# Two loads of each step issued from ScalarE's queue, earlier in the step, instead of from SyncE's

## The reference

```python
xn = layernorm(x)                       # over the 256 columns, no scale or shift
x = x + attention(xn) + ffn(xn)
# attention: 16 heads of 16; segments of 512 rows; keys and values are every 8th row
# of a segment (64 keys); for each block of 64 queries the maximum over the block is
# subtracted per key, then exp; num = w @ v, den = sum(w) + 1e-10; out = (num/den) @ Wout.T
# ffn: relu(xn @ W1 + b1) @ W2 + b2, with an inner width of 1024
```

## Time and profile before

| | |
|---|---|
| median of 3 runs | 1063.42 us (1061.55 to 1066.39) |
| the profiled execution, its own time | 1065.93 us |
| its span, first to last instruction | 1064.1 us |
| granted TensorE clock, mean | 0.998 |
| TensorE busy | 1041.9 us, 98% |
| VectorE busy | 841.3 us, 79% |
| ScalarE busy | 648.2 us, 61% |
| GpSimd busy | 623.6 us, 59% |
| share of 16 DMA engines taken by SP's queue | 73.3% |

### The profile page before, as it was taken

One profiled execution on the slowest core, in us unless ns is written; L12 is line 12 of the kernel. 1 busy time (PEld: TensorE's weight loads), 2 busy tenths in 40 slices (PEclk: granted clock), 3 DMA queues, 4 the chain that ended last, 5 costly groups with the idle time before them and its releaser, 6 DMA issues.

```text
span 1064.1 us, 19176 instructions
## 1 busy us (share of the span) xinstructions
PE 1041.9 (98%) x5381; PEld 810.6 (76%) x5381; DVE 841.3 (79%) x1465; ACT 648.2 (61%) x1080; POOL 623.6 (59%) x489
## 2 busy tenths in 40 slices
PE   5999999999999999999999999999999999999998
PEld 4676787777787777877777877777877777877777
DVE  7878888878887788888878788788877878887753
ACT  5656666666656566565666656666666665656663
POOL 6346556656656556556655656565565565556564
PEclk9999999999999999999999999999999999999999
DMA  5457777778776878777778877778768787767754
GB/s 193 98 156 207 210 214 206 206 215 227 222 209 184 228 202 244 211 194 198 214 224 225 221 204 196 219 214 235 216 191 214 202 232 211 212 176 217 196 145 146
DMA packets 153577, 216.38 MB, mean 203 GB/s; under 512 B 27345, under 2 KB 96721, under 8 KB 153553
## 3 DMA queue, kind: packets, MB, share of 16 engines
q1 hardware_dynamic: 153408, 215.96, 73.3%
q10 hardware_dynamic: 144, 0.13, 0.0%
HBM read 100.41 MB, written 58.46 MB: 149 GB/s over the span
## 4 chain that ended last, share of the span: by engine, by line
PE 88%; DVE 4%; DMA 3%; SPq 2%; issue 1%; ACT 1%; DVEq 0%; ACTq 0%
PE h_bank L1027 38%; PE y_bank L1027 38%; PE s_banks L1102 5%; PE misc L1209 3%; PE s_banks L1209 2%; PE misc L1027 2%; DMA k_pack<-k_dram 1%; DMA w_exp<-w 1%; DVE xn L828 1%; DVE s_max L845 1%; SPq L382 1%; DVE w_exp L851 1%; DMA yt_dram<-y_mem 0%; DVE q_lo L894 0%; SPq L407 0%
## 5 line engine op out<-in xcount | busy, mean ns | idle before, releaser
L540 POOL TENSOR_TENSOR h_lo<-h_full,h_hi 128x512 fp32r<-128x512 f32 x256 | 337.4, 1319 | 376.0 <-ACT h_full L621 372.6
L627 ACT ACTIVATE w_exp<-w_exp 128x512 f32<-128x512 f32 x256 | 161.6, 633 | 252.7 <-DVE w_exp L851 251.0
L619 ACT ACTIVATE h_hi<-h_bank,b_cols 128x512 fp32r<-128x512 f32 x256 | 174.8, 683 | 65.3 <-PE h_bank L1027 59.5
L1027 PE MATMUL h_bank<-xt_hi,w_hi 128*128 128x512 f32 x512 | 206.3, 403 | 0.0
L1027 PE MATMUL h_bank<-xt_lo,w_hi 128*128 128x512 f32 x512 | 199.9, 391 | 0.0
L1027 PE MATMUL h_bank<-xt_hi,w_lo 128*128 128x512 f32 x512 | 199.6, 390 | 0.0
L845 DVE TENSOR_REDUCE s_max<-s_banks 128x8 f32<-128x512 f32 x254 | 170.9, 673 | 29.1 <-PE s_banks L1102 28.8
L1027 PE MATMUL y_bank<-h_hi,w_hi 128*128 128x512 f32 x496 | 193.6, 390 | 0.2 <-ACT w_exp L627 0.2
L1027 PE MATMUL y_bank<-h_hi,w_lo 128*128 128x512 f32 x496 | 193.3, 390 | 0.0
L1027 PE MATMUL y_bank<-h_lo,w_hi 128*128 128x512 f32 x496 | 193.3, 390 | 0.0
L851 DVE TENSOR_TENSOR w_exp<-s_banks,s_max 128x512 f32<-128x512 f32 x254 | 175.7, 692 | 11.0
(11 more groups left out here) (141 smaller groups left out, 1538.5 us busy)
## 6 DMA issues: line engine op xcount, KB each, us to landing
q_pack<-q_hi SPq DMA_DIRECT2D x248, 128.0 KB, 2.5
rden_rows<-rden_dram SPq DMA_DIRECT2D x128, 128.0 KB, 4.6
x_b<-x SPq DMA_DIRECT2D x32, 512.0 KB, 4.6
x_raw<-x SPq DMA_DIRECT2D x31, 512.0 KB, 4.8
q_pack<-q_lo SPq DMA_DIRECT2D x124, 128.0 KB, 2.4
yt_dram<-y_mem SPq DMA_DIRECT2D x124, 128.0 KB, 3.5
y_mem<-yt_dram SPq DMA_DIRECT2D x31, 512.0 KB, 4.5
out<-x_b SPq DMA_DIRECT2D x31, 512.0 KB, 3.1
```

The costliest lines, as they stand in the source:

```text
L540: pool.tensor_tensor(h_part[1][:, i % HBUF], h_full[:, i % HBUF], f32(h_part[0][:, i % HBUF]), ALU.subtract).then_inc(h_lo, 1)
L619: act.activation(h_part[0][:, i % HBUF], h_bank[i % 2][:], ACT.Relu, bias=b1_cols[:, i:i + 1]).then_inc(h_hi, 1)
L627: act.activation(w_exp[:, pair], w_exp[:, pair], ACT.Exp).then_inc(w_ready, 1)
L1027: mm = pe.matmul(ps, stationary[a], moving[b], start=start and c == 0 and n == 0, stop=stop and c == len(pairs) - 1 and n == 2, skip_group ...
```

## The change

The loads of x for statistics (`load_x` and `load_keys` of the steps) and for the residual (`load_again`) leave SP's list and are issued by ScalarE on its own DMA queue: `load_next` after `hidden` at i = 3, `load_again` after `hidden` at i = 6. In the last step `load_again(31)` stands at i = 3; before, SP issued it at the end of step 30. GpSimd's `residual(31)` moves from i = 3 to i = 6. The loads of the first and lead step stay with SP. What each load waits for is the same as before.

```diff
 (SyncE)
-            def load_again(s, par):
-                sp.wait_ge(y_stored[par], (s - par) * 8)
-                sp.dma_start(x_b2[:, par], x_rows[s]).then_inc(x_again[par], 16)
...
-                if load:
-                    sp.wait_ge(xn_ready, s + 2)
-                    load_x(s + 3, 1 - par)
-                if load and par == 1:
-                    sp.wait_ge(xn_keys_ready, s + 3)
-                    load_keys(s + 3)
...
-                if ffn and not by_rows(s):
-                    load_again(s, par)
...
-                if attention and not norm:
-                    load_again(s + 1, 1 - par)
 (GpSimd)
-                    if i == 3 and by_rows(s):
+                    if i == 6 and by_rows(s):
                         residual(s, par)
 (ScalarE)
+            def load_next(s, par):
+                act.wait_ge(xn_ready, s + 2)
+                act.dma_start(x_raw[:, 1 - par], x_rows[s + 3]).then_inc(x_loaded[1 - par], 16)
+                if par == 1:
+                    act.wait_ge(xn_keys_ready, s + 3)
+                    act.dma_start(x_keys[:], x_key_rows[bass.ds((s + 3) * KEYS, P)]).then_inc(x_keys_loaded, 16)
+
+            def load_again(s, par):
+                act.wait_ge(y_stored[par], (s - par) * 8)
+                act.dma_start(x_b2[:, par], x_rows[s]).then_inc(x_again[par], 16)
...
                     if i in first:
                         hidden(past(s), first[i])
+                    if i == 3 and load:
+                        load_next(s, par)
+                    if i == (3 if by_rows(s) else 6):
+                        load_again(s, par)
```

## The result

The changed kernel takes 1097.07 us, the median of 4 runs (1090.75 to 1100.16), beside 1063.3 us for the kernel before in the same series. The ratio is 1.0291, with a 95% interval from 1.0264 to 1.0318. That is 33.8 us more (31 us by the ratio), where 1.5 us less was forecast, and far above the range's 1068.5 us. The profiled execution of after took 1090.75 us (span 1088.8 us, mean granted clock 0.994), the lowest of its four, so its rows show less of the loss than the median: 24.7 us of span.

What follows compares the result with a forecast made beforehand. TensorE bounds the kernel (88% of the span), so gains come only from idle time or clock. From the 1063.42 us median, 1.5 us off k_pack's waits and 0 elsewhere gave 1061.9 us, range 1058 to 1068.5.

Steps and rivals of the forecast that it cites:

- the new place of the transfers: Odd steps: x_raw and x_keys beside the store and xt_dram put off xt_dram's landing 0.8 to 1.6 us; worth 0.
- the cover: Slack in odd steps, 0.7 us before xt_hi plus 1.0 us before the first query product; TensorE feels delay from 1.7 us.
- The reload's early place: ScalarE at i = 6, ahead of k_hi: an issue of 0.4 to 0.6 us fits a 1.46 us wait; worth 0.
- Step 0: x_raw at 48 us instead of 54 meets q_pack, with TensorE idle around its keys; 0, up to +1 us.
- the loads put off the transposed rows: Rival, odd steps: xt_dram's delay stalls TensorE 0.4 to 1.2 us a step, 1075 us; 12% chance.
- The rule of turns between queues: DMA engines take queues in turn by packet, so xt_dram gets half a full engine while x_raw lasts; 1075 us.
- ScalarE's issue: Each load's issue on ScalarE takes 0.4 to 0.6 us, at most 1.47, and fits in its waits; worth 0.
- SP's 26 us: 75 load issues leave SP's queue, some 26 us of SP's time, which buys nothing by itself; worth 0.
- k_pack's waits: TensorE's 2.3 us of waits for k_pack shrink with two loads gone from before it; 1.5 us gained, 2.3 at best.
- The last step: residual between hidden_lo 6 and 7 leaves 0.6 us of cover; worth 0, bound +0.5 us.
- the sign by which it would be seen wrong: ScalarE's xt_hi waiting for xt_raw instead of for TensorE in odd steps would show the forecast wrong.

Runs made afterwards that it cites:

- e1: Changed kernel with the reload (x_b) back on SP at its old place, so only x_raw and x_keys are early on ScalarE; 1068.87 us, ratio 1.0047.
- e2: Changed kernel with x_raw and x_keys back on SP at their old places, so only the reload is early on ScalarE; 1074.97 us, ratio 1.0093.
- e5: Changed kernel with the reload moved from i = 6 to behind transposed_hi, which waits for xt_raw; 1070.52 us, ratio 1.0059.
- e13b: Changed kernel with the reload behind pair_keys_hi and a real wait for k_hi ahead of its issue; 1074.18 us, ratio 1.0086.
- e14b: Changed kernel with only x_keys (128 KB per odd step) back on SP behind xt_raw; 1067.41 us, ratio 1.0030.
- e4: Changed kernel with all loads still on ScalarE's queue but issued at about their old times, by waits for xt_dram's landing and k_lo; 1065.64 us, ratio 1.0017.
- e15: Changed kernel with x_keys and both loads of step 0 back on SP at their old places; 1064.15 us, ratio 0.9993.
- e16: Kernel before, with only x_raw's loads from step 1 on issued by ScalarE at i = 3; 1061.86 us, ratio 0.9975.
- e6: Changed kernel with ScalarE issuing the loads in even steps alone, SP as before in odd steps; 1067.57 us, ratio 1.0029.
- e11: All loads on SP's one queue, x_raw and x_keys ahead of xt_dram and the reload ahead of xt_raw; 1096.80 us, ratio 1.0299.
- e8: Changed kernel with a padded x_raw tile, so its loads go in pieces of 1 KB instead of 4 KB; 1091.28 us, ratio 1.0239.
- e7: Changed kernel with ScalarE issuing the loads in the odd steps alone; 1085.23 us, ratio 1.0207.
- e3: All loads on SP's one queue but early, x_raw and x_keys ahead of xt_dram and the reload right behind xt_raw; 1076.99 us, ratio 1.0116.
- e9: Changed kernel with the reload placed one instruction later in the program, behind pair_keys_hi, without a wait; 1095.79 us, ratio 1.0236.

## Why the prediction was wrong

**The step that failed** is the one on the new place of the transfers: "What does not fit, 0.8 to 1.6 us, puts off xt_dram's landing", "TensorE feels it from 1.7 us on, and the estimate stays just below. x_raw no longer runs beside xt_raw, which helps", "Worth 0". The delay itself was sized rightly, at the upper end: 1.6 us measured (5.00 to 6.61 us). That 1.6 us by itself stays within the cover is right as well: e1, with the same delay, loses 1.3 us at the query products in the whole kernel. What the step left out is what xt_raw then runs beside. The prediction moved x_b from 415.31 to about 410.2 in its own text, and xt_raw by up to 1.6 us from 407.49 to 409.1, and never set the two side by side. It also took an issue on ScalarE to start when the activation before it ends. The reload was issued 1.02 us ahead of k_hi, which is 409.14 on the old timeline, and so they meet, 0.56 us apart at most. xt_raw's landing, which it took as a constant 3.8 us, became up to 6.8 us, and both covers, 0.7 and 1.0 us, were used up. That x_raw no longer runs beside xt_raw didn't help: in e1's odd steps xt_raw lands in 3.9 us (median), in 3.7 before. That this meeting on top of the delay carries most of the loss is shown from five sides: the halves alone sum to 16.7 of 33.8 us (e1, e2), taking the reload away leaves 6.0 (e5), making it really later leaves about 10 (e13b), making xt_raw earlier under an unmoved reload leaves 3.4 (e14b), and a meeting with xt_raw on time costs 2.1 (e4).

**The reload's early place** was costed at nothing by way of its issue alone. Its bytes cost too: e2 shows 11.4 us through rden_rows, yt_dram and k_pack, transfers of which the prediction asked only whether something was taken from before them, not whether something was put there. But that price belongs to a reload beside the rows at their old place, and isn't a part of the 33.8 us: with x_raw early as well, and the meeting avoided, the early reload costs nothing that can be measured against before (e15), and some 2 us beside e16, which differs from e15 in the reload and the last step's residual (0.9975 against 0.9993, their intervals overlap).

**Step 0** was allowed 0 to +1 us and measured +2.8 us in q_pack's wait alone, 3 to 4 us by e6 and by e14b against e15. This is a term mis-sized, and the reason stood in the text ("x_raw at 48 us instead of 54 meets q_pack").

**The rival "the loads put off the transposed rows"** had the right chain (xt_dram, xt_raw, xt_hi, the query products in odd steps) and 12%. Its price, 0.4 to 1.2 us a step from a longer delay of xt_dram, was too low (18 us in the 13 odd steps of after's loop, up to 3.4 us in one), and its mechanism was not the whole: the xt_dram delay makes four tenths of the lateness in a stalled step (1.51 of 3.81 us in step 9), xt_raw's own landing the rest. The rule of turns between queues that stood beside it (the Trainium skill, DMA: Bandwidth & Descriptors, Queues, rings and completion order) is not needed for a late landing: e11's even steps have one on a single queue, where the reload stands ahead. And e8's store and xt_dram land no sooner for the smaller pieces beside them.

**What held.** ScalarE's issue is cheap: 0.34 us each, and less than its price in time, since here it starts while the hidden activation runs (342.31 against 342.18 to 342.87) and the exponential behind it still waits 2.39 us, as before. SP's 26 us buy nothing (e4). k_pack's waits go, 2.3 us (e16 cashes it). The last step costs nothing: from its last xt_hi to the end of the span are 69.6 us, 69.9 before. The forecast also named the sign by which it would be seen wrong, xt_hi waiting for xt_raw in odd steps, and that is what the trace has.

**What stays open.** Why some tenths of a microsecond between two issues decide over 1.6 us of landing. It also doesn't say why 3 us ahead cost only 0.3 us in e11's odd steps. Open too are the 10 us by which e6 and e7 fall short of the whole, and e8's longer matmuls.

## What to carry to other kernels

When a load is moved to an earlier place, write down for each late-bound transfer when it will be issued after the change and what will be in flight beside it, with all moved transfers at their new times at once; costing each against the old timeline finds neither half of this loss. Measure a delay from the event that starts the chain, here VectorE's z, and not from the chain's first DMA, or a late first DMA hides (e3). Where a chain of two dependent DMAs has 1 to 2 us of cover and its first link is already being put off, keep a 512 KB load from going out ahead of or together with the second: put it behind by a semaphore, not by its place in the program. And move one load at a time: here one of three was worth 2.8 us, and in the whole change 14 small loads decided over 30.

## What was unexpected of the hardware

- A 512 KB load issued between 0.35 us ahead and 0.22 us behind another made that other's data usable 1.6 us later on average than one issued 0.22 us or more behind. Another load, 0.13 us behind, did the same in 13 steps out of 13 (e4: 5.5 us on average).
- 128 KB more in an odd step's busiest stretch put xt_raw's issue back by 0.97 us (5.64 us in e14b, 6.61 in after), about the time of 128 KB at some 135 GB/s, although the core's DMA engines stood at a mean share of 0.77 over the loop.
- ScalarE issued a DMA 1.02 us before an activation that stands ahead of it in the program (e9).
- Two of the ten stalls in after's loop, 2.4 and 3.4 us long, were followed by 3.4 us at the lower clock, with means of 0.74 to 0.84 over windows of 4 us; one of 2.8 us was not. TensorE's busy time grew by 6.2 us over the kernel for the same matmuls; how much of it is the clock isn't measured.
